# Transposed one-hot tiles of a graph network on one Trainium2 core: compared from resident row numbers instead of stored and loaded

## The reference, cut to what matters

```python
def _gat(x, src, dst, ew, Wg, att_s, att_d, bias, n):
    h = (x @ Wg).reshape(n, HEADS, HID)
    a_s = jnp.einsum('nhc,hc->nh', h, att_s)
    a_d = jnp.einsum('nhc,hc->nh', h, att_d)
    logits = jax.nn.leaky_relu(a_s[src] + a_d[dst] + ew[:, None], NEG_SLOPE)
    m = jax.ops.segment_max(logits, dst, num_segments=n)
    ex = jnp.exp(logits - m[dst])
    denom = jax.ops.segment_sum(ex, dst, num_segments=n)
    alpha = ex / denom[dst]
    ...
x = _layernorm(x + gat_stack(x, edges), axis=-1)
x = _layernorm(x + gcn_gcn(x, edges), axis=-1)
x = _layernorm(x + gcn(x, edges), axis=-1)
x = _layernorm(x + sage_sage(x, edges), axis=-1)
```

## Time and profile before

| what | us |
|---|---|
| median of 3 runs | 5085.48 |
| lowest, highest | 5083.7, 5086.98 |
| span of the profiled execution | 5076.4 |
| stage: start of the program to the node chain | 0 to 94 |
| stage: slots | 956 to 1219 |
| stage: pass one, first gather to last `delta` | 1239 to 1611 |
| stage: pass two, first gather to last `delta` | 2032 to 2327 |
| stage: pass 3a | 2744 to 2926 |
| stage: pass 3b | 2948 to 3085 |

### The profile page before, as it was taken

The page is one execution under the profiler, slowest core; times in us unless marked ns, Lnnn a source line. Parts: engine busy times, 40 slices in busy tenths (PEclk is TensorE's granted clock), DMA queues, the critical chain, the costliest instruction groups (busy, mean ns, idle before and its releaser), DMA issues. The chain is left out here.

```text
span 5076.4 us, 107540 instructions
## 1 busy us (share of the span) xinstructions
PE 3921.6 (77%) x23992; PEld 2865.7 (56%) x23992; DVE 3818.0 (75%) x14850; ACT 3446.1 (68%) x11317; POOL 3017.8 (59%) x2914
## 2 busy tenths in 40 slices
PE   2999999565997798994998974997876676665554
PEld 1666766344775455773555752444765565665554
DVE  5899999676998787887886966997768787444443
ACT  0899999554886576784776863887878787333332
POOL 2888888475552122661223452887757676767777
PEclk9999999788998899997999997998999898997666
DMA  2566666587997576994776984775766566543332
GB/s 63 162 186 199 199 194 193 175 288 242 351 349 250 180 239 205 338 354 160 233 241 230 350 290 156 225 227 171 230 205 212 189 204 190 155 145 116 93 101 70
DMA packets 606699, 1061.18 MB, mean 209 GB/s; under 512 B 109737, under 2 KB 130875, under 8 KB 606509
## 3 DMA queue, kind: packets, MB, share of 16 engines
q1 hardware_dynamic: 524780, 920.61, 53.0%
q0 software_dynamic: 81728, 138.51, 10.7%
HBM read 608.75 MB, written 453.92 MB: 209 GB/s over the span
## 5 line engine op out<-in xcount | busy, mean ns | idle before, releaser
L2534 POOL DMA_INDIRECT got_c<-table,src_row x980 | 930.4, 949 | 387.6 <-issue 295.6
L1428 POOL DMA_INDIRECT src_got_s<-table,src_row x588 | 554.6, 943 | 452.9 <-PE bank L1474 105.1
L2566 PE MATMUL bank<-pick_c,got_c 128*128 128x128 f32 x1960 | 327.7, 319 | 349.6 <-DMA got_c<-table,src_row 271.2
L2076 PE MATMUL bank<-w_all,dt_m 128*128 128x512 f32 x1176 | 567.7, 599 | 35.0 <-DMA dt_m<-delta_t 33.4
L2566 PEld LDWEIGHTS bank<-pick_c,got_c 128*128 128x128 f32 x1960 | 284.2, 223 | 392.5 <-issue 233.5
L2050 POOL TENSOR_TENSOR part_m<-part_m,half_sum_m 128x512 f32<-128x512 f32 x98 | 158.7, 1619 | 580.3 <-DVE half_sum_m L2283 580.3
L1601 ACT ACTIVATE z_s<-z_s,shift_s,dev_s 128x128 f32<-128x128 f32 x1080 | 444.2, 486 | 1.8 <-DVE shift_s L1739 1.3
L791 PEld LDWEIGHTS bank<-w_mean,ht 128*128 128x128 f32 x2352 | 312.4, 193 | 142.9 <-issue 142.9
L2590 PE MATMUL bank<-w_c,agg_c 128*128 128x128 f32 x1960 | 365.4, 311 | 5.0 <-ACT agg_c L2711 4.7
L2711 ACT COPY agg_c<-bank 128x512 f32<-128x512 f32 x245 | 142.6, 582 | 325.4 <-DVE bank L1914 277.8
L788 PE MATMUL bank<-bias,first_row 128*128 128x512 f32 x588 | 321.8, 629 | 38.7 <-ACT ht L851 13.8
(11 more groups left out here) (352 smaller groups left out, 11925.4 us busy)
## 6 DMA issues: line engine op xcount, KB each, us to landing
table<-rows SPq DMA_DIRECT2D x294, 256.0 KB
x_s<-table SPq DMA_DIRECT2D x270, 256.0 KB
x_c<-table SPq DMA_DIRECT2D x245, 256.0 KB
table<-z_s SPq DMA_DIRECT2D x196, 256.0 KB
table<-z_c SPq DMA_DIRECT2D x196, 256.0 KB
table<-mid_s SPq DMA_DIRECT2D x172, 256.0 KB
own_rows_s<-table SPq DMA_DIRECT2D x147, 256.0 KB
pick_t_s<-picks_t SPq DMA_DIRECT2D x147, 256.0 KB
```

The source lines that it names most:

```text
L1428: nc.gpsimd.indirect_dma_start(out=src_got[r][:, g, :], out_offset=None, in_=tables[l].rows, in_offset=bass.IndirectOffsetOnAxis(ap=src_ro ...
L2076: nc.tensor.matmul(b_h[k % n_h][:, :], dt[b.slot][:, k, :], w_all[:, l, :, :].rearrange("p h d -> p (h d)"), start=True, stop=True).then_i ...
L2534: nc.gpsimd.indirect_dma_start(out=got[r][:, g, :], out_offset=None, in_=t_in.rows, in_offset=bass.IndirectOffsetOnAxis(ap=src_row[:, t:t ...
L2566: ins = nc.tensor.matmul(b_sum[r][:, k * P:(k + 1) * P], got[b.slot][:, k, :], pick[r][:, k, :], start=k == 0, stop=sage, skip_group_check ...
```

## The change

Instead of storing the transposed one-hot tiles once and loading them in each score pass, the kernel keeps all 25088 keys as bytes in every partition (`keys`, 128 x 25088 uint8) and a column with the partition's own number (`row_of`), and makes each batch's `pick_t` by one compare of 128 x 512: on POOL in passes one and three, on DVE in pass two.

```diff
+        key_row = nc.dram_tensor("key_row", (1, n_slots), U8, kind="Internal").ap()
+        row_of = sb("row_of", [P, 1])
+        keys = sb("keys", [P, n_slots], U8)
...
-                n_load = 13
+                n_load = 14
...
+                        sp.dma_start(row_of[:, :], io["row_of"]).then_inc(loaded, 16)
...
+                        sp.wait_ge(keys_made, 1)
+                        sp.dma_start(key_row[0, :].rearrange("(q e) -> q e", q=rq), key_bytes[:, :]).then_inc(keys_out, 16)
+                        sp.wait_ge(keys_out, 16)
+                        sp.dma_start(keys[:, :], key_row.to_broadcast([P, n_slots])).then_inc(keys_in, 16)
...
+                        nc.vector.tensor_copy(key_bytes[:, :], kr[:, :]).then_inc(keys_made, 1)
...
-                                sp.wait_ge(pick_t_made, b.count(1, 1))
-                                sp.sem_inc(sp_pace, 1)
-                                sp.dma_start(turned_batch(picks_t, b), pick_t[r][:, :]).then_inc(pick_t_stored[r], 16)
...
-                                    pool.wait_ge(pick_t_made, b - 4)
+                                    pool.wait_ge(pick_made, b - 3)
...
-                                pe.wait_ge(pick_made, b.count(1, 1))
-                                hold(pe, pick_t_made, b.count(1, 0))
-                                for g in range(GB):
-                                    ins = nc.tensor.transpose(bank[4][:, g * P:(g + 1) * P], pick[b.slot][:, g * P:(g + 1) * P], ident[:, :])
-                                ins.then_inc(picks_turned, 1)
...
-                                act.wait_ge(picks_turned, b.count(1, 1))
-                                hold(act, pick_t_stored[b.slot], b.ring4(16, -16))
-                                nc.scalar.copy(pick_t[b.slot][:, :], bank[4][:, :]).then_inc(pick_t_made, 1)
...
-                        def load_picks(b):
-                            hold(sp, spread_made, b.count(1, -3))
-                            sp.sem_inc(sp_pace, 1)
-                            sp.dma_start(flat(pick_t[b.slot]), turned_batch(picks_t, b, start)).then_inc(pick_in[b.slot], 16)
...
+                        def build_picks(b):
+                            if b > 3:
+                                pool.wait_ge(spread_made, b - 3)
+                                pool.sem_inc(pool_pace, 1)
+                            at = (start + b) * (GB * P)
+                            nc.gpsimd.tensor_scalar(flat(pick_t[b % 4]), keys[:, at:at + GB * P], row_of[:, 0:1], None,
+                                                    ALU.is_equal).then_inc(picks_made, 1)
+                        if l != 1:
+                            pool.wait_ge(keys_in, 16)
                         for b in range(n_part):
                             r = b % 4
+                            if l != 1:
+                                build_picks(b)
                             for g in range(GB):
...
-                            pe.wait_ge(pick_in[r], b.ring4(16))
+                            pe.wait_ge(picks_made, b.count(1, 1))
...
+                        def build_picks(b):
+                            hold(dve, spread_made, b.count(1, -3))
+                            dve.sem_inc(dve_pace, 1)
+                            nc.vector.tensor_scalar(flat(pick_t[b.slot]), keys[:, bass.ds((b.batch() + start) * (GB * P), GB * P)],
+                                                    row_of[:, 0:1], None, ALU.is_equal).then_inc(picks_made, 1)
```

More of the change, by code:

```diff
@@ L10 @@
 I32 = mybir.dt.int32
+U8 = mybir.dt.uint8
 ALU = mybir.AluOpType
@@ L172, in program @@
         iota = sb("iota", [P, P])
+        row_of = sb("row_of", [P, 1])
+        keys = sb("keys", [P, n_slots], U8)
+        keys_in = ctx.enter_context(nc.semaphore("keys_in"))
         eps = sb("eps", [P, 1])
@@ L327, in edge_structure @@
                 map_def = s("map_def", [P, n_rows_nodes // P, 4])
-                loaded, chain, to_pe, turned, map_out, iotas = (sem(x) for x in (
-                    "loaded", "chain", "to_pe", "turned", "map_out", "iotas"))
-                n_load = 13
+                loaded, chain, to_pe, turned, map_out, iotas, keys_made, keys_out = (sem(x) for x in (
+                    "loaded", "chain", "to_pe", "turned", "map_out", "iotas", "keys_made", "keys_out"))
+                n_load = 14
                 with nc.Block() as block:
@@ L1037, in first_slots @@
                 xt, hidden = pairs("slot_xt"), pairs("slot_hidden")
-                ht, rows, pick, pick_t = (fours(n) for n in ("slot_ht", "slot_rows", "slot_pick", "slot_pick_t"))
+                ht, rows, pick = (fours(n) for n in ("slot_ht", "slot_rows", "slot_pick"))
                 x = [c.enter_context(nc.sbuf_tensor(f"slot_x{r}", [P, GB, D], F32)) for r in range(4)]
@@ L1232, in fours @@
                     return [s(f"{name}{r}", [P, GB, D]) for r in range(4)]
-                src_got, own_rows, pick_t, dt = (fours(n) for n in ("src_got", "own_rows", "pick_t", "dt"))
-                delta = pairs("delta")
+                src_got, own_rows, dt = (fours(n) for n in ("src_got", "own_rows", "dt"))
+                delta, pick_t = pairs("delta"), fours("pick_t")
                 scores = pairs("scores", (P, P))
@@ L1252, in edge_scores @@
                 bias_set = [sem(f"bias_set{h}") for h in range(2)]
-                dt_stored, own_in, pick_in = ([sem(f"{n}{r}") for r in range(4)] for n in ("dt_stored", "own_in", "pick_in"))
+                dt_stored, own_in = ([sem(f"{n}{r}") for r in range(4)] for n in ("dt_stored", "own_in"))
+                picks_made, pool_pace = sem("picks_made"), sem("pool_pace")
                 sc_stored = [sem(f"sc_stored{r}") for r in range(2)]
```

16 lines of the change are left out of this document (9 added, 7 removed).

## The result

The changed kernel takes 5118.47 us (median of 5 runs, 5116.25 to 5156.98) against 5085.48 (5080.72 to 5086.98): 33 us more, ratio 1.0081 with a 95% interval of 1.0064 to 1.0099. The direction was forecast; the size was not, 5118 lies above the range's end of 5116, and the sum had +11.8 us.

The account below looks back on a forecast made before the run. DVE was taken to bound passes one and 3a (pass three's first part), the DMA queue pass two, POOL's gathers 3b (its second part). 0.7 - 2.5 + 0 + 6.3 + 0 + 7.3 = +11.8 us gave 5097 us, range 5084 to 5116.

Parts of the forecast that it names:

- The bound of passes one and 3a: Pass one and pass three's first part: DVE sets the pace at 7.5 us a batch; DMA engines are full but not late.
- the 0: Pass one and pass three's first part: POOL has room for the compare, 0 us, between -10 and +5.
- Pass two: DVE's compare replaces the wait for the store of `scores`: +7.6 us, less 1.3 at the start, +6.3, between +2 and +15.
- 3b: the step that failed: Second part of pass three: POOL's compare, taken as 1.0 us, lengthens its gather queue, +7.3 us; at 1.27 us +14.
- its duration less 0.12: Pass three's second part: a POOL operation between gathers costs its length less 0.12 us, so 0.88 us for the compare.
- the formula: Pass three's second part: first gather plus 24 batches of 5.92 us less 0.3, landing 3.0 us later, then `delta`: +7.3 us.
- The rival that came true: Pass three's second part: POOL's compare is a generic routine of 1.6 us, 14 us more, 5111 us in all; chance 0.15.
- The lock between DVE's compare and gathers: Pass two: gathers block DVE's compare on the shared SBUF path, 0.30 us a batch, +14 us, 5111 in all; chance 0.12.
- the +5 end of the term for passes one and 3a: Pass one and pass three's first part: up to +5 us if POOL's compare meets DVE's `shift`, which has two SBUF inputs.
- Slot stage: Without transposes, copies and stores of the tiles, mainly the drain after the last gather shortens: -2.5 us, between -5 and 0.
- The start: First stage: one more small load and a conversion cost +0.7 us; the 25 KB store and 3.2 MB broadcast load are hidden.
- The offset: Whole kernel: the profiled span of 5076.4 us lies 9.1 us under the median 5085.48; this difference was carried over.

Follow-up runs that it names:

- experiment 8: The changed kernel with every compare on DVE, in all passes: 5121.36 us, ratio 1.0070 to the kernel before.
- experiment 1: The changed kernel with ten single POOL operations over 128x512, each four times, ahead of its first stage: 5627.01 us, on a chip where the kernel before takes 5638.57.
- Experiment 9: The changed kernel with POOL's compare in the second part of pass three cut to two of four tiles, the others zeros: 5104.25 us, ratio 1.0040.
- experiment 14: The kernel before plus only the resident row numbers, all tiles still loaded and nothing compared: 5085.44 us, ratio 0.9997.
- experiment 5: The changed kernel run again without an edit: 5126.19 us, ratio 1.0085 to the kernel before.
- Experiment 15: The kernel before plus resident row numbers, with POOL comparing in pass one and the first part of pass three, other tiles loaded: 5094.26 us, ratio 1.0018.
- experiment 11: Experiment 7 plus POOL compares in pass one and pass three's first part, and only even batches' tiles turned and stored: 5079.95 us, ratio 0.9989.
- experiment 7: The kernel before plus resident row numbers, POOL comparing odd batches in pass two, DVE comparing in pass three's second part: 5081.37 us, ratio 0.9993.

## Why the prediction was right or wrong

*The bound of passes one and 3a.* Right in what decides: a tenth less traffic, and pass one keeps its 359.8 us; 0.49 us more on DVE is paid in full in pass one (experiment 8). For 3a the 0 was 1.6 us short.

*Pass two.* Right in mechanism and period. DVE's compare was 487 ns (510 forecast), the period 6.14 us on average (6.11), ACT's wait for `scores` left. From first to last `delta` the stage costs 294.7 - 288.0 = +6.7 us with five executions on either side, where the sum had +7.6. Ahead of the first `delta` 1.3 us were to be saved, and 0.2 were; from the first gather on it is 304.5 - 298.0 = +6.5 against the +6.3 forecast. That they come so near is in part luck, since these two terms miss by 0.9 and 1.1 us in opposite directions. The +9.1 of the two first profiles was a short execution of the loaded stage.

*3b: the step that failed.* "Nearest are a counter fill ... and above it the two-input operation ... I take 1.0: it reads one tensor more than the fill and one less than the other." The number of tensors read doesn't order POOL's operations: the one-input operation with a scalar takes 1.59 us. Nor was 1.27 a bound, since the trace of before has the two-input operation at a median of 1.64 us in 98 instances (experiment 1). The rest of the working holds but for a small term, "its duration less 0.12": between gathers the compare costs its full length, 6.59 - 4.99 = 1.60 us. With 6.58 us a batch the formula gives 2947.6 + 24 x 6.58 - 0.3 + 3.0 = 3108.2, +23.1 us, and the stage got 22.9 us longer. That is 15.6 us of the miss of 21, some 14 of them the 0.59 us by which the price was short. Experiment 9, with the operation at the assumed size, cost 6.

*The rival that came true* had this size and place ("24 x 0.6 = 14 us more") and a chance of 0.15. The text bounded the unseen operation from above by 1.27 us, yet allowed 1.6 for a generic routine in its rivals, without a row for it; the two should have been one bound, with the chance spread over it. Even that rival's 5111 is 7 us under the result; the rest is in the small terms and in what stays open, below.

*The lock between DVE's compare and gathers* did not show: 487 ns in pass two beside gathers; an SBUF path shared with POOL's own compare did, on `shift`, as the +5 end of the term for passes one and 3a had it.

*Slot stage.* The drain is shorter by 2.5 us in the first two profiles, as forecast. Over all executions the gap from the last gather to pass one is 47.1 us with the turned tiles stored (six, 45.4 to 48.7) and 45.9 without (six, 45.2 to 46.9): -1.2.

*The start.* +0.7 forecast, 0 within 5 us measured (experiment 14).

*What stays open.* By stages the change costs 22.9 + 6.7 + 1.6 (3a) - 1.2 = 30 us, against 33 in the result's runs and 41 in experiment 5. Experiment 15 puts 9 us on POOL's compares in passes one and 3a, where stages show under 3. Some of the rest is in the last stage, convolve, whose code is untouched: its 196 indirect stores of `out_dram` take 11 ns longer each. The tile view of `out_dram` in experiments 14 and 15:

```profile
L2590 POOL DMA_INDIRECT out_dram<-z_c,slot_node x196: 971/972/1018, 4612.9 to 5082.8; - x196
L2590 POOL DMA_INDIRECT out_dram<-z_c,slot_node x196: 982/984/1031, 4615.8 to 5087.1; - x196
```

It is so in every profiled execution, on all chips: in the twelve where POOL compares anything the median is 984 to 986 ns, in the five where it compares nothing 972 to 975. From the first store to the last it is 471.3 to 472.3 us (nine executions on chips with 5085) against 469.0 to 469.9 (four), and the program ends with them: 2.2 us. How a compare that ended 1.5 ms earlier reaches these stores isn't shown. Convolve as a whole takes 1562.3 to 1569.2 us in the executions with POOL's compares in passes one and 3a (eight) and 1560.9 to 1563.9 in the others (five). The ranges overlap, and experiment 11, which has the same compares, isn't slower than experiment 7, which lacks them in these passes. So some 32 of the 33 us have a place, and about 5 of experiment 15's 9 have none.

*The offset.* The prediction carried the 9.1 us between span and median over as if it were the kernel's. It is the luck of one execution: the second had its span 9 us above its median.

## What to carry to other kernels

Removing traffic pays only in the stage that waits for it, and the work put in its place must go to an engine with room in that same stage: here DVE had room in 3b and POOL in passes one and 3a, pass two had room on POOL for every second batch, and the change had pass two and 3b the other way. An operation that a trace has never shown on an engine is bounded by the slowest of its size there (here 1.64 us, in the trace all along), not by counting its inputs, or measured first; and a difference of a few microseconds between two profiled executions is held against a second execution of the same program before it is called a cost.

## What the runs showed of the hardware

- POOL's operation with one input and a scalar takes 1.56 us for 128x512 at best, for uint8, bfloat16 and float32 input alike, add or compare; a converting copy takes 0.61. The two-input operation of that size has a median of 1.27 us at one place of the program and 1.64 at another. DVE does the same compare from uint8 in 0.45 to 0.49.
- Between POOL's gathers an operation costs its length: four gathers take 4.99 us, with a compare of 0.94 us 5.94, with one of 1.59 us 6.59.
- Indirect stores issued by POOL took 984 to 986 ns in the twelve profiled executions whose POOL had done such compares, 972 to 975 in the five others. The cause isn't shown.
- The same program took 5085 us on some chips and 5638 on another. On that one pass two moved 286 GB/s instead of 343, and comparing on DVE instead of loading won 15 us in that stage where it cost 7 on the others: the sign of such a change can depend on the chip.
- Two profiled executions of one program on chips where it takes 5085 us differed by 17 us in span, among it 12 us ahead of the slot stage.
